# The last stage's sum of a row and its norm made by ScalarE from two numbers per row

## The reference, cut to what matters

```python
# graph layer: gather rows of support by src, weigh, add up by dst
x = x + gnn(layernorm(x))
# _layernorm: (x - mean) / sqrt(var + 1e-5)
t = layernorm(x)                      # 12500 x 256
logits = t @ router_w.T               # 8 experts
rw, re = top_k(softmax(logits), 2)    # weights made to sum to one
out = t                               # the MoE starts from its tokens
for e in range(8):
    h = gelu(t @ w1[e] + b1[e])
    out = out + combine[:, e] * (h @ w2[e] + b2[e])
x = x + out                           # so: x + t + experts
```

## Time and profile before

| | us |
|---|---|
| median of 3 runs | 4567.17 |
| lowest and highest of them | 4557.66, 4570.12 |
| the profiled execution: own time | 4560.52 |
| the profiled execution: span | 4558.8 |
| busy in the span: PE, DVE, ACT, POOL | 3883.7, 3687.5, 3231.1, 3026.4 |
| the last stage, first gather to end | 2111 to 4558.8 |

### The profile page before, as it was taken

One profiled execution on the slowest core, in us unless ns is written; L12 is line 12 of the kernel. 1 busy time (PEld: TensorE's weight loads), 2 busy tenths in 40 slices (PEclk: granted clock), 3 DMA queues, 4 the chain that ended last, 5 costly groups with the idle time before them and its releaser, 6 DMA issues.

```text
span 4558.8 us, 88999 instructions
## 1 busy us (share of the span) xinstructions
PE 3883.7 (85%) x28087; PEld 3382.1 (74%) x28087; DVE 3687.5 (81%) x10149; ACT 3231.1 (71%) x6837; POOL 3026.4 (66%) x3177
## 2 busy tenths in 40 slices
PE   1688888888888889985689988999889988998998
PEld 1688888788767777774468777777777877787788
DVE  8799888889778888885668888878887888878886
ACT  3799988889878778774356666666666666666665
POOL 0466676677756566653777777777777777777751
PEclk6799999999999999996579999999999999999999
DMA  7798888888799899976434444444444444444431
GB/s 229 279 327 322 326 317 321 321 316 292 290 336 327 310 331 327 326 270 183 131 108 124 118 116 121 115 125 116 122 116 125 115 116 121 116 124 116 116 97 41
DMA packets 323818, 928.88 MB, mean 204 GB/s; under 512 B 50896, under 2 KB 132896, under 8 KB 320848
## 3 DMA queue, kind: packets, MB, share of 16 engines
q0 software_dynamic: 153216, 483.15, 31.8%
q1 hardware_dynamic: 167960, 426.60, 28.4%
q10 hardware_dynamic: 2172, 13.35, 0.8%
HBM read 597.06 MB, written 325.83 MB: 202 GB/s over the span
## 4 chain that ended last, share of the span: by engine, by line
PE 35%; DVE 20%; DMA 15%; ACT 12%; issue 9%; POOL 8%; SPq 1%; ACTq 0%; DVEq 0%; POOLq 0%
POOL X L1284 7%; DMA X<-h,tabT 7%; PE ps L1433 6%; PE ps L1454 5%; DMA msgd<-A,tabT 4%; PE ps L1230 3%; DVE S L1194 3%; ACT A L868 3%; PE ps L1323 3%; DVE low L1198 2%; DMA L<-msgd 2%; PE ps L803 2%; PE ps L772 2%; PE ps L1013 2%; PE ps L804 2%
## 5 line engine op out<-in xcount | busy, mean ns | idle before, releaser
L1284 POOL DMA_INDIRECT X<-h,tabT x1620 | 1602.0, 989 | 595.3 <-issue 374.2
L1312 ACT ACTIVATE gH<-X,tabT 128x256 fp32r<-128x256 f32 x1080 | 533.0, 506 | 518.9 <-DMA X<-h,tabT 498.8
L868 ACT ACTIVATE A<-ps,A 128x256 f32<-128x256 f32 x1856 | 746.0, 521 | 74.2 <-PE ps L804 73.1
L917 POOL DMA_INDIRECT msgd<-A,tabT x464 | 567.7, 1224 | 318.0 <-ACT A L868 218.1
L1301 DVE SCALAR_TENSOR_TENSOR gL<-X,tabT,gH 128x256 fp32r<-128x256 f32 x1080 | 515.5, 477 | 209.3 <-ACT gH L1312 206.8
L1296 DVE TENSOR_SCALAR s<-iota,tabT 128x125 fp32r<-128x125 f32 x1800 | 572.3, 335 | 0.8
L803 PE MATMUL ps<-winH,DT 128*128 128x256 f32 x1856 | 508.8, 306 | 52.0 <-issue 40.7
L1325 PE MATMUL ps<-gH,s 128*125 128x256 f32 x1200 | 399.8, 334 | 106.1 <-ACT gH L1312 72.1
L804 PE MATMUL ps<-winL,DT 128*128 128x256 f32 x1856 | 469.4, 285 | 0.0
L1323 PE MATMUL ps<-X,s 128*125 128x256 f32 x1080 | 364.5, 421 | 115.7 <-ACT X L1308 65.2
L803 PEld LDWEIGHTS ps<-winH,DT 128*128 128x128 f32 x1856 | 358.8, 193 | 69.3 <-issue 55.9
(11 more groups left out here) (272 smaller groups left out, 10965.8 us busy)
## 6 DMA issues: line engine op xcount, KB each, us to landing
L<-msgd SPq DMA_DIRECT2D x200, 650.0 KB, 6.2
L<-msgd SPq DMA_DIRECT2D x200, 520.0 KB, 6.2
A<-sbd SPq DMA_DIRECT2D x58, 805.0 KB, 6.5
msgd<-A SPq DMA_DIRECT2D x100, 390.0 KB
X<-h,tabT POOLq DMA_INDIRECT x1620, 2.8
winR<-h SPq DMA_DIRECT2D x116, 128.0 KB
A<-in_x SPq DMA_DIRECT2D x10, 1120.0 KB
h<-A ACTq DMA_DIRECT2D x10, 1120.0 KB
```

Source lines behind the costliest of these rows:

```text
L868: e.activation(M[:, n, 0:F], psum[4 + v % 4][:, (n % 2) * F:(n % 2 + 1) * F], ACT.Identity, scale=M[:, n, F + 2:F + 3]).then_inc(evc, 1)
L917: e.indirect_dma_start(msgd, bass.IndirectOffsetOnAxis(ap=idxI[g % 4][:, t:t + 1], axis=0), msg[g % 3][:, t * 4 * RW:(t + 1) * 4 * RW], No ...
L1284: e.indirect_dma_start(B.G[c % GRL], None, h2, bass.IndirectOffsetOnAxis(ap=tab3[:, c, 0:1].bitcast(I32), axis=0)).then_inc(gatl[c % GRL], 16)
L1312: e.activation(B.gH[c % HR2][:, :], B.G[c % GRL], ACT.Identity, scale=w_).then_inc(g_hi, 1)
```

## The change

DVE no longer adds the two arrays. The sum x + (x - m) r, with m the mean and r the reciprocal deviation of a row, is x (1 + r) - m r. DVE makes the two numbers 1 + r and -m r per row (n values each, for 125 partitions), right behind the norm, and ACT makes the sum from `xt` alone with one Identity activation per block (scale 1 + r, bias -m r), behind its four copies of the transposes. The buffer `v` grows by 8 numbers.

```diff
@@ -343,7 +343,7 @@
         st_o = [sem(f"st_o{k}") for k in range(4)]
         ld_ex, wsp = sem("ld_ex"), sem("wsp")
         d2_tr, d2_cp, d2_z, d2_x1, d2_v, d2_sq, d2_t, d2_o = (sem(n) for n in ("d2_tr", "d2_cp", "d2_z", "d2_x1", "d2_v", "d2_sq", "d2_t", "d2_o"))
-        d2_tt, d2_tc, tsp, d2_lg, rt_l, rt_s, rt_e, rt_c = (sem(n) for n in ("d2_tt", "d2_tc", "tsp", "d2_lg", "rt_l", "rt_s", "rt_e", "rt_c"))
+        d2_tt, d2_tc, tsp, d2_lg, d2_k, rt_s, rt_e, rt_c = (sem(n) for n in ("d2_tt", "d2_tc", "tsp", "d2_lg", "d2_k", "rt_s", "rt_e", "rt_c"))
         d2_ct, d2_cc, d2_b2, d2_o2 = (sem(n) for n in ("d2_ct", "d2_cc", "d2_b2", "d2_o2"))
         l1s, gel, hhi, hlo, l2s, moe = (sem(n) for n in ("l1s", "gel", "hhi", "hlo", "l2s", "moe"))
         one_way = ExitStack()
@@ -1475,7 +1475,7 @@
 
             def first(i, tick):
                 b0, n = SBS[i]
-                v, rt, TT = small[0:R, 570:594], B.rt, B.tT
+                v, rt, TT = small[0:R, 570:598], B.rt, B.tT
                 if i == 0:
                     e.wait_ge(wsp, 4 * WP)
                 for k in range(2):
@@ -1502,6 +1502,11 @@
                     c_ = slice(k * 512, k * 512 + n * R)
                     e.activation(TT[:, c_], bank(i, "tt", k)[:, 0:n * R], ACT.Copy).then_inc(d2_tc, 1)
                     e.activation(B.tH[i % 2][:, c_], bank(i, "tt", k)[:, 0:n * R], ACT.Copy).then_inc(d2_tc, 1)
+                e.wait_ge(d2_k, 2 * (i + 1))
+                for j in range(n):
+                    c_ = slice(j * F, (j + 1) * F)
+                    m = e.activation(B.Z(i)[:, c_], B.xt[:, c_], ACT.Identity, bias=v[:, 24 + j:25 + j], scale=v[:, 20 + j:21 + j])
+                m.then_inc(d2_o, 1)
                 tick()
                 yield
                 p8 = rt[:, 8:8 + 8 * n]
@@ -1575,7 +1580,7 @@
             def first(i, tick):
                 b0, n = SBS[i]
                 Zs, X, C, rt = B.Z(i), B.xt, B.comb[i % 2], B.rt
-                v = small[0:R, 570:594]
+                v = small[0:R, 570:598]
                 tick()
                 yield
                 e.wait_ge(ld_xt, 32 * (i + 1))
@@ -1602,11 +1607,11 @@
                     m = e.tensor_scalar(Zs[:, j * F:(j + 1) * F], X[:, j * F:(j + 1) * F], v[:, 2 * j:2 * j + 1], v[:, 16 + j:17 + j],
                                         ALU.subtract, ALU.mult)
                 m.then_inc(d2_t, 1)
+                e.tensor_scalar(v[:, 20:20 + n], v[:, 16:16 + n], 1.0, None, ALU.add).then_inc(d2_k, 1)
+                e.scalar_tensor_tensor(v[:, 24:24 + n], v3[:, 0:n, 0], -1.0, v[:, 16:16 + n], ALU.mult, ALU.mult).then_inc(d2_k, 1)
                 tick()
                 yield
-                e.wait_ge(d2_t, i + 1)
                 e.wait_ge(d2_tt, 2 * (i + 1))
-                e.tensor_tensor(Zs[:, 0:n * F], X[:, 0:n * F], Zs[:, 0:n * F], ALU.add).then_inc(d2_o, 1)
                 e.wait_ge(d2_tc, 4 * (i + 1))
                 if i >= 2:
                     e.wait_ge(l1s, 16 * (i - 1))
```

## The result

The changed kernel takes 4556.57 us in the median (4548.13 to 4566.0, 20 runs) beside 4567.61 (4556.03 to 4572.69, 20 runs) of the kernel before on the same chip: ratio 0.998, interval 0.9974 to 0.9986; the medians are 11.0 us apart. The ratio and its interval come from all executions of both kernels and not from the two medians alone, so the two can differ: 0.998 is some 9 us. Forecast were 4556 us and 10.7 less. The profiled execution took 4553.19 us.

The account below looks back on a forecast made before the run. The prediction took POOL's back-to-back gathers as the last stage's clock, with PE the bound only in the last 225 us. Terms -12.1 + 0.5 + 0 + 0.9 = -10.7 took 4567.2 to 4556 us; range 4544 to 4569.

Parts of the forecast that it names:

- The held gathers: Last stage: 20 gathers begun during a wide L1609 lose their stretching, -12.1 us, bounds 0 and 12.1.
- Rival 1: At the sum: its place doesn't matter to the gathers, by the skill's rule or a stretching neighbour; 4569 us, chance 0.13.
- The small instructions: DVE's two new instructions of 4 numbers per group hold some gathers: +0.5 us, bounds 0 and 8.6.
- what else stretches gathers: Remaining stretching in the last stage, from L1301 above all: taken as 0, bounds -5 to +10 us.
- rival 2: ACT's burst delays DVE, whose L1301s run closer together and meet more gathers: +10 us, 4566 us, chance 0.08.
- the 52 us of stretching: Last stage: gathers' mean 989 ns over median 957, times 1620, on the stage's clock; some 40 us stay.
- ACT's burst in the middle: New Identity activations, 45 us of ACT time, fit into its idle time behind the copies: 0, bounds 0 and 41.
- Rival 4: Wide groups' `first`: ACT becomes what the buffers wait for, 41 us added; 4598 us, chance 0.04.
- The end: Last group: two activations ahead of the Exp chain move PE by 0.95 us: +0.9 us, bounds 0 and 3.8.
- the three groups before: Groups ahead of the last: gathers and ACT's waits lie between, DVE has less to do; taken as 0.
- The sum: All terms together: -12.1 + 0.5 + 0 + 0.9 = -10.7 us, giving 4556 us.

Follow-up runs that it names:

- e7: The changed kernel with the sum back on DVE at its old place, as four instructions reading x1 alone: 4561.4 us, ratio 0.9977.
- e11: The kernel before with DVE's two-input sum L1609 cut into one instruction per block: 4559.89 us, ratio 0.9975.
- e6: The kernel before without L1609, nothing in the sum's place, so x1 is missing in its output: 4556.66 us, ratio 0.9972.
- e9: The changed kernel with ACT's activations for the sum behind the Exp in place of ahead of it: 4558.32 us, ratio 0.9971.

## Why the prediction was right

- **The held gathers, -12.1 us.** Right in its mechanism: the same sum with one input gives the gain without moving anything off DVE (e7), and cutting the instruction gives most of it (e11). The two traces before had 12.6 and 14.6 us of it; in the changed kernel the gathers at the low parts have none. Rival 1 is out. The prediction read the hold a little too simply, though: a gather that begins just ahead of the instruction isn't held (3852.18), so it matters which of the two begins first, and not only what runs 0.12 us after the gather's start. The prediction carried as a rival what the Trainium skill's page "SBUF — State Buffer", section "Who interferes with whom", says of a `tensor_tensor`: that it was not seen to stall DMAs. The runs show 0.53 us more per gather, and up to 1.74 us in place of 0.96 in the trace before, so this doesn't hold for gathers of this kind. But the same section says that a DVE instruction with two inputs in SBUF contends with a GpSimd instruction that reads SBUF. The gather does read there: its row numbers come from the buffer `tabT`, as its rows say (`X<-h,tabT`). By that sentence the hold was to be expected, and the prediction was wrong to count the whole rule against the gain. That it is the reading of the row numbers which is held, no run shows.
- **The small instructions, +0.5 us, and what else stretches gathers, 0.** The small instructions cost nothing that shows: the seven gathers that begin just ahead of them in the two traces kept their length. The middle lost 10.5 us where 12.1 - 0.5 = 11.6 were forecast, but in other parts: the sum had held gathers there for 12.1 and 13.8 us, and L1301 stretched them by 31.2 and 32.3 us before and by 35.0 and 35.3 after, +3.4. The other five kernels have 30.3 to 33.3. So rival 2 may hold for some 3 us and not for 10; a cause isn't shown. Also, the 52 us of stretching leave out the 180 gathers into `W1s`; with them it is 56.4, and some 44 stay in place of 40.
- **ACT's burst in the middle, 0.** Right. It took 1.97 us in place of 1.8, POOL's waits stayed at 0.3, ACT's waits for gathers shrank by 45 us (41 forecast), and the kernel without any sum (e6) has the same middle. Rival 4 is out.
- **The end, +0.9 us.** The mis-sized term. PE's wait grew by 0.7, near the 0.9, but I priced the wait alone. Behind a wait of 2.5 us TensorE ran at its lower clock level for 3.4 us more, which cost another 1.5. And for the three groups before I took 0, but PE came to the last wait 3.6 us late already; the last store was 1.0 us longer, too. The end of both traces came out 6.75 us longer, though 3.8 was the bound that I had put on it. That ACT's activations are behind it is made likely by the ends of 298.2 to 299.4 us without them (e6, e7, e11) or with them behind the Exp (e9), in one trace each; how they make the 3.6 us isn't shown.
- **The sum, -10.7 us.** That it met the -11.0 so closely is luck: by the traces' own parts, -10.5 and +6.75, it would be -4, the ratio stands for -9, and the second timing of the same kernel, -6.9 us, lies between. Whether the clock falls at the end of the executions that weren't profiled, I can't tell from these runs; so I leave open how much of the 6.75 us is in the timed 4556.57.

Of the kernels tried, `e9_act_behind_exp_2` has the lowest ratio, 0.9971, but neither it nor e7 (0.9977) or e11 (0.9975) can be told from the changed kernel. For the gain it was not needed to move the sum to ACT.

## What to carry to other kernels

If one engine does nothing but start transfers back to back, look at how long each start takes, and at which instructions of other engines run where one is long: what counts then is not how busy the other engine is but how long each single instruction is that holds a start, here those with two SBUF inputs, so drop an input or cut the instruction, and look at the trace for whether the new form holds too. Ask in which condition that engine is the clock at all; where it waits for buffers, the same edit is worth nothing. Near the end, where nothing else covers PE, a wait that grows by 0.7 us can cost three times that through the clock that follows it (2.1 us here).

## What the runs showed of the hardware

- An indirect gather of 128 rows of 256 numbers took 0.957 us of POOL and went out every 1.26 us. One that met a DVE instruction with two inputs in SBUF ended 0.83 us after that instruction's end: L1609, its pieces, and L1301 alike. A `tensor_scalar` with one input in SBUF, on the same data, added 0.02 us, but a CAST with one input (L1547, 0.69 us) held gathers in the same way. Gathers begun 0.03 to 0.09 us ahead of an L1301 weren't held.
- Two matmul streams with the same work ran 36 and 28 instructions in 5 us, at a granted clock of 1.00 and 0.66, behind waits of 1.79 and 2.50 us. In nine traces the clock fell behind both waits of 2.5 us at this place and behind none of the seven of 1.81 or less; one group earlier, behind waits of 2.04 to 2.10 us, it fell in five of the nine.
- The same kernel took 4567.6 to 4572.5 us in four comparisons and 4977.1 in a fifth. The last stage of the four kernels traced there was 2831 to 2845 us long; in the nine other traces it was 2435 to 2452.
